# Sorting the tokens of a mixture-of-experts layer in two halves, with gathers and weight loads inside one block loop

## Chip, cores and metric

The kernel runs on one core of one Trainium2 chip. The metric is the time on the device in microseconds (us), median of the runs shown. All arithmetic of the layers is float32. P is 128 throughout.

## What is computed

Sixteen samples x of 128 tokens by 128 features pass through four layers. Cut to the core:

```python
# layer 0: an expert per sample, chosen by an id (8 experts, 128 -> 512 -> 128)
h = gelu(x[b] @ Wi[e] + bi[e]);  r = h @ Wo[e] + bo[e] + x[b]
x = layer_norm(r) * gamma[e] + beta[e]
# layer 1: norm, then norm over tokens scaled and shifted per sample (from a small hypernetwork),
# then a mixture of 8 experts (128 -> 512 -> 128), two per token, added to x
h = film(norm_tokens(layer_norm(x) * ln_g + ln_b))
probs = softmax(h @ router_w);  gates, idx = top_k(probs, 2);  gates /= gates.sum()
x = x + sum_over_k(gates[k] * (relu(h @ w1[idx[k]] + b1[idx[k]]) @ w2[idx[k]] + b2[idx[k]]))
# layer 2: pairs of features rotated by theta and phi of the sample
# layer 3: 128 -> 32, gelu, a 32x32 matrix chosen by an id, 32 -> 128, residual, layer_norm
```

## The kernel before

Four groups of four samples run through layer 0: TensorE multiplies (up, gelu on ScalarE, down), VectorE takes mean and variance, GpSimd raises the variance to the power -0.5 and does scale and shift, VectorE normalises. Norm and film of layer 1 for one group run beside layer 0 of the next. Then logits and the two largest per token (`top2`) on VectorE.

All 2048 tokens, 4096 token-and-expert pairs, are sorted by expert at once: a matmul ranks the pairs (`p_rank`), a scan on VectorE gives each pair a slot, each expert's slots are padded to whole blocks of 128, and a matmul of one-hot tiles (`hot_in`, `hot_blk`) inverts the table: for each of 39 blocks, which row of h goes to which slot (`src_i`), and where its result goes (`dest_i`).

A block is: GpSimd gathers 128 rows of h by index out of device memory (`gather`, line 496, ring of 8, seven ahead), TensorE transposes them (line 869), VectorE copies the transpose and the expert's w1 from a table in SBUF (lines 1285, 1291), TensorE does four up matmuls (two instructions each), ScalarE four relu activations (line 651), TensorE four down matmuls, VectorE adds b2 (line 1298), GpSimd scatters the 128 result rows to their token's place (`scatter`, line 504). Instructions of every matmul helper carry line 710.

When all scatters have landed, eight transfers of 256 KB bring the rows back, two per group. VectorE combines them with the gates and x (lines 1333, 1341), and layer 3 follows group by group, with its variance power on GpSimd (line 519) and the output stored by SyncE. Every engine runs its own list in the order written; semaphores alone join them. The order around the blocks on GpSimd:

```python
            for n in range(AHEAD):
                gather(n)
            for n in range(BLOCKS):
                if n + AHEAD < BLOCKS:
                    gather(n + AHEAD)
                scatter(n)
```

## Time and profile before

| | us |
|---|---|
| median of 3 runs | 268.74 (265.86 to 272.72) |
| span of the profiled execution | 237.1 |
| TensorE busy in it | 187.1 |
| VectorE | 127.9 |
| GpSimd | 125.8 |
| ScalarE | 100.3 |

The record holds no time of the profiled execution itself, only its span, from the first to the last instruction; the median is 31.6 us above that. Busy shares are averages over stages with different limits. Matmuls are pipelined and their ends are modelled, so a busy TensorE is not one at its peak.

### The profile page before, as it was taken

How to read it: one execution, taken by the hardware profiler on the slowest of the kernel's cores; microseconds unless marked ns; L12 is line 12 of the kernel's file. 1: busy time of each engine (PE TensorE's matmuls, PEld its weight loads, DVE VectorE, ACT ScalarE, POOL GpSimd, SP SyncE). 2: the span in 40 equal slices, each digit the busy share in tenths (PEclk: the TensorE clock that was granted, in tenths of full speed). 3: DMA queues.
4: the chain of work that ended last, by engine and by line, in shares of the span. 5: the costliest groups of instructions: out<-in, count | busy, mean ns of one | idle time of the engine just before them, and what ended most of it. 6: DMA issues, size and time to landing. Idle time of an engine off the chain costs nothing.

```text
span 237.1 us, 5140 instructions
## 1 busy us (share of the span) xinstructions
PE 187.1 (79%) x1247; PEld 157.3 (66%) x1248; DVE 127.9 (54%) x540; ACT 100.3 (42%) x297; POOL 125.8 (53%) x133
## 2 busy tenths in 40 slices
PE   6699696998446593989999898888997999789900
PEld 5699495996343462478998787777776884268700
DVE  6101425679977699635776555553332320378761
ACT  3123169568221339135555434444443343025530
POOL 6002363655655002577777777777777774001960
PEclk9999889999755555599999999999999999979955
DMA  5999968931169910011111111111112310940113
GB/s 181 234 340 324 305 182 247 333 112 48 52 204 322 318 44 1 24 47 55 48 49 53 49 44 48 49 55 44 45 56 43 52 43 0 251 106 1 44 44 88
DMA packets 32790, 27.19 MB, mean 115 GB/s; under 512 B 3561, under 2 KB 28282, under 8 KB 32768
## 3 DMA queue, kind: packets, MB, share of 16 engines
q1 hardware_dynamic: 23648, 18.44, 26.1%
q0 software_dynamic: 2496, 4.66, 7.6%
q10 hardware_dynamic: 6624, 3.85, 5.7%
q8 instruction: 8, 0.13, 0.2%
q14 instruction: 14, 0.11, 0.1%
HBM read 22.73 MB, written 4.65 MB: 116 GB/s over the span
## 4 chain that ended last, share of the span: by engine, by line
PE 25%; POOL 22%; issue 17%; DMA 16%; DVE 15%; ACT 3%; ACTq 1%; DVEq 0%; POOLq 0%
PE bank L710 22%; POOL got L496 9%; DMA x_sb<-in_x 9%; POOL expert_rows L504 9%; DMA got<-h_rows,src_i 4%; DVE z L1058 2%; DMA w_place<-expert_rows 2%; POOL rstd L453 2%; DVE nmr L1361 2%; PE bank L717 1%; DVE hot_in L1190 1%; ACT act L597 1%; POOL rs L519 1%; DVE hot_blk L1188 1%; DVE st L1349 1%
## 5 line engine op out<-in xcount | busy, mean ns | idle before, releaser
L651 ACT ACTIVATE rows<-bank,small 128x128 f32<-128x128 f32 x156 | 44.5, 368 | 54.3 <-PE bank L710 54.3
L496 POOL DMA_INDIRECT got<-h_rows,src_i x39 | 38.8, 994 | 18.0 <-issue 9.7
L710 PE MATMUL bank<-gotT,rows 128*128 128x128 f32 x312 | 43.7, 283 | 5.6 <-issue 4.0
L504 POOL DMA_INDIRECT expert_rows<-rows,dest_i x39 | 39.9, 1022 | 12.4 <-issue 11.7
L710 PEld LDWEIGHTS bank<-gotT,rows 128*128 128x128 f32 x312 | 37.8, 191 | 10.8 <-issue 8.3
L710 PE MATMUL bank<-w,rows 128*128 x312 | 43.1, 282 | 1.2 <-issue 0.6
L710 PEld LDWEIGHTS bank<-w,rows 128*128 128x128 f32 x312 | 37.8, 191 | 2.8 <-issue 1.6
L597 ACT ACTIVATE act<-bank,small 128x128 f32<-128x128 f32 x64 | 18.1, 370 | 25.5 <-PE bank L710 25.3
L1298 DVE TENSOR_TENSOR rows<-bank,b_tab 128x128 f32<-128x128 f32 x39 | 11.4, 291 | 31.3 <-PE bank L710 30.3
L453 POOL TENSOR_TENSOR rstd<-veps,minus_half 128x4 f32<-128x4 f32 x12 | 12.3, 1022 | 25.5 <-DVE veps L1048 14.5
L1285 DVE COPY gotT<-bank 128x128 f32<-128x128 f32 x39 | 11.2, 288 | 17.5 <-PE bank L869 17.2
L710 PE MATMUL bank<-w_place,act 128*128 128x128 f32 x128 | 19.2, 298 | 1.4 <-ACT act L597 1.4
L710 PE MATMUL bank<-xT,w_place 128*128 128x128 f32 x128 | 20.0, 308 | 0.0
L710 PEld LDWEIGHTS bank<-xT,w_place 128*128 128x128 f32 x128 | 18.7, 224 | 0.7 <-issue 0.7
L710 PEld LDWEIGHTS bank<-w_place,act 128*128 128x128 f32 x128 | 17.3, 209 | 1.8 <-ACT act L597 1.8
L1291 DVE COPY rows<-w 128x512 f32 x39 | 17.6, 451 | 0.7 <-issue 0.7
L519 POOL TENSOR_TENSOR rs<-ve,minus_half 128x4 f32<-128x4 f32 x4 | 4.1, 1022 | 20.2 <-DVE ve L1354 20.1
L869 PE MATMUL bank<-ident,got 128*128 128x128 f32 x39 | 11.5, 294 | 3.1 <-DMA got<-h_rows,src_i 2.8
L710 PE MATMUL bank<-w,ident 128*128 128x512 f32 x26 | 13.9, 692 | 0.0
L710 PE MATMUL bank<-small,hT 128*128 128x8 f32 x32 | 5.7, 306 | 9.5 <-ACT hT L579 9.5
L1039 DVE BATCH_NORM_STATS2 st<-bank 128x6 f32<-128x128 f32 x32 | 7.1, 284 | 10.8 <-PE bank L710 9.0
L710 PEld LDWEIGHTS bank<-small,hT 128*128 128x128 f32 x32 | 5.5, 260 | 10.3 <-issue 10.3
(197 smaller groups left out, 263.5 us busy)
## 6 DMA issues: line engine op xcount, KB each, us to landing
w_place<-in_l_wi SPq DMA_DIRECT2D x16, 256.0 KB, 4.9
w_place<-in_l_wo SPq DMA_DIRECT2D x16, 256.0 KB, 5.9
w<-in_exp_w SPq DMA_DIRECT2D x16, 256.0 KB, 5.9
rows<-in_l_rows SPq DMA_DIRECT2D x16, 192.0 KB, 5.9
x_sb<-in_x ACTq DMA_DIRECT2D x4, 256.0 KB, 6.4
h_rows<-h_row ACTq DMA_DIRECT2D x4, 256.0 KB, 2.5
w_place<-expert_rows SPq DMA_DIRECT2D x4, 256.0 KB, 5.6
w_place<-expert_rows ACTq DMA_DIRECT2D x4, 256.0 KB, 6.3
```

Of the source, the lines that this page charges most:

```text
L453: g_.tensor_tensor(rstd[:, kind, :], veps[:, kind, :], minus_half[:, 0:GS], ALU.pow)\
L496: g_.indirect_dma_start(got[:, n % RING, :], None, h_dram, bass.IndirectOffsetOnAxis(ap=src_i[:, n:n + 1], axis=0))\
L504: g_.indirect_dma_start(y_dram, bass.IndirectOffsetOnAxis(ap=dest_i[:, n:n + 1], axis=0), y_blk[:, n % 4, :], None, bounds_check=TOPK * NR ...
L519: g_.tensor_tensor(rs3[:, g % 2, :], ve3[:, g % 2, :], minus_half[:, 0:GS], ALU.pow)\
L597: last = a_.activation(act0[:, b % 2, c, :], bank[1 + b % 2][:, c * P:(c + 1) * P], ACT.Gelu, bias=cols[:, bass.ds(e * FC + (R_BI + c), 1)])
L651: last = a_.activation(hid[:, k % 2, c, :], bank[k % 2][:, c * P:(c + 1) * P], ACT.Relu, bias=cols[:, bass.ds(e * FC + (R_B1 + c), 1)])
L710: return t_.matmul(out_, lhsT, rhs, start=start, stop=stop)
L869: t_.transpose(bank[6 + k % 2][:, 0:P], got[:, k % RING, :], ident[:]).then_inc(p_gT, 1)
L1039: do(v_.bn_stats(st[:, kind, k, :], src(k)))
L1285: v_.tensor_copy(gotT[:, n % 2, :], bank[6 + n % 2][:, 0:P]).then_inc(v_gT, 1)
L1291: v_.tensor_copy(w1_now[:, n % 2, :], w1[:, bass.ds(expert[n], 1), :].rearrange("p o f -> p (o f)"))\
L1298: v_.tensor_tensor(y_blk[:, n % 4, :], bank[4 + n % 2][:, 0:D], b2_tab[:, bass.ds(expert.pop(n), 1), :].rearrange("p o d -> p (o d)"), ALU ...
```

## The change

The tokens of samples 0 to 7 and of 8 to 15 become two halves. Each is sorted by itself, with half the rank and one-hot widths, into 23 blocks: 46 in all, for 39. The first half's norm, film, routing and sort are placed between the layer-0 samples of groups 2 and 3; the second half's between the blocks of the first (the `if k ==` steps below; a step k is up of block k, down of block k-1, transpose of block k+2). The normalisation of layer 0 moves wholly to VectorE, scale and shift included, in two passes. The bias of layer 0 comes through a matmul on transposed x. The x loads are issued earlier, and weights, output weights and rows of layer 0 have semaphores of their own.

A block's w1 is fetched from device memory by SyncE, five blocks ahead, into a ring of six; it was copied on VectorE. Its transpose is copied by ScalarE. Its result goes by a plain store of SyncE to its slots; there is no scatter. Later each sample's two rows per token are fetched by an indirect transfer through the slot of the token, two per sample, 32 in all: 16 for the first half between the second half's blocks, 16 behind the last block. Gathers and these fetches are held back until TensorE has done the up matmuls or the transpose of a given step. The table of the inverse (one-hot tiles) is made ahead of the row store and the sine on ScalarE. Layer 3 of the first half runs inside the block loop; the second half in four units of two samples; its per-sample matrices come from a table of 18. The variance power of the last unit uses ScalarE's square root and a Newton step on VectorE. GpSimd no longer scales and shifts the output. The loops with a hardware counter are written out. The warming matmuls ahead of layer 3 go.

```diff
+    HALVES = 2
+    HB = NB // HALVES
+    HG = NG // HALVES
+    KT = TOPK * HB
+    BL = (TOPK * HB * S + E1 * (P - 1)) // P
+    NBLK = HALVES * BL
...
+    RING, YRING, TRING, WRING = 16, 4, 3, 6
+    LEAD = 4
+    BOTH = BL - 4
+    FIRST_ROWS = BL + 2
+    WARM_START = (4, 3, 4)
+    UNITS = [(GS * g, GS) for g in range(HG)] + [(b, 2) for b in range(GS * HG, NB, 2)]
+    NU = len(UNITS)
...
+                load_w0(b)
+                if b == 5:
+                    load_rows0(0)
+                if b == 8:
+                    load_rows0(1)
+                if 11 <= b < 15:
+                    load_w2((b - 11) * E1 // 4, (b - 10) * E1 // 4)
+                if b == 13:
+                    load_rows0(2)
...
+            def load_w1(n):
+                e = sp.value_load(exp_i[0:1, n:n + 1], min_val=0, max_val=E1 - 1)
+                if n >= WRING:
+                    sp.wait_ge(p_u, n - WRING + 1)
+                sp.dma_start(w1_now[:, n % WRING, :], exp_w1[bass.ds(e, 1)].rearrange("o d f -> d (o f)"))\
+                    .then_inc(l_w1[n % WRING], 16)
+            def store_y(n):
+                sp.wait_ge(v_y, n + 1)
+                m = n % BL
...
+            for k in range(NBLK):
+                if k + WRING - 1 == BL:
+                    sp.wait_ge(v_exp, 2)
+                if k >= 1:
+                    store_y(k - 1)
+                if k + WRING - 1 < NBLK:
+                    load_w1(k + WRING - 1)
...
+            def fetch_row(u, t, k):
+                h, j = t // HB, k * HB + t % HB
+                g_.indirect_dma_start(y_in[:, t // GS, k, t % GS, :], None, y_dram[h],
+                                      bass.IndirectOffsetOnAxis(ap=slot_i[:, h, j:j + 1], axis=0))\
+                    .then_inc(l_y[u], 16)
...
+            def beside_up(k):
+                pool.wait_ge(p_u, k + 1)
+            def beside_rows(k):
+                pool.wait_ge(p_gT, min(k + 3, NBLK))
...
+            for n in range(BL):
+                if n >= LEAD:
+                    beside_up(n - LEAD)
+                if n == BOTH:
...
+                    pool.wait_ge(st_h[2], 16)
+                    pool.wait_ge(st_h[3], 16)
...
+                if n > BOTH:
+                    beside_rows(n - LEAD)
+                    gather(BL + n - BOTH - 1)
...
+            ahead = 2 * BL - BOTH - 1
+            first_half = rows_of(0) + rows_of(1)
+            for k in range(BL - LEAD, NBLK - LEAD):
+                if k == FIRST_ROWS:
+                    stored(0)
+                i = k - FIRST_ROWS
+                gathers = 2 if i < 0 else k % 2 if i < 11 else 1
+                if gathers > 0 and ahead < NBLK:
+                    beside_up(k)
+                    gather(ahead)
+                    ahead += 1
+                if gathers > 1 and ahead < NBLK:
+                    beside_rows(k)
+                    gather(ahead)
+                    ahead += 1
+                if 0 <= i < len(first_half):
+                    beside_rows(k)
+                    fetch_row(*first_half[i])
...
+            stored(1)
+            fetch(2)
+            power3(1)
+            fetch(3)
+            fetch(4)
+            power3(2)
+            fetch(5)
+            power3(3)
+            power3(4)
...
+                if k == 0 and g + 2 < NG:
...
+                if b == 10:
+                    film_h(0)
+                if b == 12:
+                    film_h(1)
+                if b == 14:
+                    store_rows(0)
...
+            transposed(0)
+            transposed(1)
+            e = block_expert(0)
+            for k in range(NBLK):
+                hidden(k, e)
+                if k + 1 == BL:
+                    act.wait_ge(v_exp, 2)
+                if k + 1 < NBLK:
+                    e = block_expert(k + 1)
+                if k + 2 < NBLK:
+                    transposed(k + 2)
+                if k == 5:
+                    film_h(2)
+                if k == 6:
+                    film_h(3)
+                if k == 7:
+                    store_rows(2)
+                if k == 8:
+                    store_rows(3)
+                if k == 11:
+                    hot_rows(1)
+                if k == 13:
+                    act.wait_ge(v_smax, 1)
+                    a_.activation(soft[:], soft_in[:], ACT.Exp).then_inc(a_sexp, 1)
...
+                if b == 11:
+                    z_transposes(1)
+                if b == 12:
+                    route(0)
+                if b == 14:
+                    rank(0)
+                    rows_back(0)
+                if b == 15:
+                    rows_back(1)
...
+                if b == 8:
+                    z_transposes(0)
+                if b == 13:
+                    route(1)
...
+            pe.wait_ge(v_l0, NG)
+            rows_T(0)
+            rows_T(1)
+            for k in range(NBLK + 1):
+                if k == BL + 1:
+                    pe.wait_ge(v_exp, 2)
+                if k >= 1:
+                    e = pe.value_load(exp_i[0:1, k - 1:k], min_val=0, max_val=E1 - 1)
+                if k < NBLK:
+                    blk_up(k)
+                if k >= 1:
+                    blk_down(k - 1, e)
+                if k + 2 < NBLK:
+                    rows_T(k + 2)
+                if k == 2:
+                    z_transposes(2)
+                if k == 3:
+                    z_transposes(3)
+                if k == 6:
+                    route(2)
+                    rows_back(2)
+                if k == 7:
+                    route(3)
+                    rows_back(3)
+                if k == 9:
+                    rank(1)
+                if k == 13:
+                    inverse(1)
+                if k == 19:
+                    experts3(2)
+                if k == 20:
+                    experts3(3)
+                if k == 37:
...
+            def l0_centre_scale(g):
+                dve.wait_ge(l_rows0[g], 16 * GS)
+                for k in range(GS):
+                    last = v_.scalar_tensor_tensor(
+                        out=z0[:, g % 2, k, :], in0=down_bank(g)[:, k * P:(k + 1) * P],
+                        scalar=mv[:, 0, g % 2, k, 0:1], in1=rows0[:, GS * g + k, 0, :],
+                        op0=ALU.subtract, op1=ALU.mult)
+                last.then_inc(v_l0, 1)
+            def l0_spread_shift(g):
+                dve.wait_ge(g_rstd[0], g + 1)
+                dve.wait_ge(v_l0, g + 1)
+                for k in range(GS):
+                    do(v_.scalar_tensor_tensor(
+                        out=x1[:, GS * g + k, :], in0=z0[:, g % 2, k, :], scalar=rstd[:, 0, g % 2, k:k + 1],
+                        in1=rows0[:, GS * g + k, 1, :], op0=ALU.mult, op1=ALU.add))
+                settle()
...
+            def last_root():
+                r, v = rs3[:, there(NU - 1)], ve3[:, there(NU - 1)]
+                dve.wait_ge(a_sd3, 1)
+                do(v_.reciprocal(r, sd3[:]))
+                settle()
+                do(v_.tensor_tensor(nr3[:], r, r, ALU.mult))
+                settle()
+                do(v_.tensor_tensor(nr3[:], nr3[:], v, ALU.mult))
+                settle()
+                do(v_.tensor_scalar(nr3[:], nr3[:], -0.5, 1.5, ALU.mult, ALU.add))
+                settle()
+                do(v_.tensor_tensor(r, r, nr3[:], ALU.mult))
+                settle()
...
+            l0_stats(0)
+            l0_centre_scale(0)
+            l0_spread_shift(0)
+            l1_stats(0)
+            l1_norm(0)
+            l0_stats(1)
+            l0_centre_scale(1)
+            l0_spread_shift(1)
+            l1_stats(1)
+            row_stats(0)
+            l1_norm(1)
+            film_gain()
+            film_factors(0)
+            row_stats(1)
+            film_factors(1)
+            l0_stats(2)
+            top2(0)
+            top2(1)
+            count_blocks(0)
+            sort_slots(0)
+            hot_blocks(0)
+            hot_slots(0, 8)
+            dve.wait_ge(p_bias, 1)
+            v_.tensor_copy(bias3[:], q_bias3).then_inc(v_bias, 1)
+            hot_slots(8, KT)
+            block_experts(0)
+            sources(0)
+            l0_centre_scale(2)
+            l0_stats(3)
+            l0_centre_scale(3)
+            l0_spread_shift(2)
+            l1_stats(2)
+            l0_spread_shift(3)
+            l1_stats(3)
+            dve.wait_ge(l_w2, 16 * (E1 + 1))
+            dve.wait_ge(v_exp, 1)
...
+                if k == 1:
+                    l1_norm(2)
+                if k == 2:
+                    l1_norm(3)
+                if k == 3:
+                    row_stats(2)
+                if k == 4:
+                    film_factors(2)
+                    row_stats(3)
+                if k == 5:
+                    film_factors(3)
+                if k == 7:
...
+                if k == 10:
+                    count_blocks(1)
+                if k == 11:
+                    sort_slots(1)
+                    hot_blocks(1)
+                if 12 <= k < 14:
+                    hot_slots(8 * (k - 12), 8 * (k - 11))
+                if k == 12:
```

## Rows read from the trace of the kernel before

**Rows 1.** The page, part 2: 40 slices, busy tenths of TensorE and its granted clock
```profile
PE   6699696998446593989999898888997999789900
...
PEclk9999889999755555599999999999999999979955
```

**Rows 2.** Waits: who waited for whom, total us, times, longest
```profile
PE bank L717 <- DMA x_sb<-in_x: 5.8, 3, 2.2
```

**Rows 3.** Timeline, TensorE: sums of groups 1 and 3 (start us, us, engine, line)
```profile
36.82 1.02 PE L710 MATMUL bank<-x_bo,ident 128*128 128x512 f32 x2
...
58.07 1.02 PE L710 MATMUL bank<-x_bo,ident 128*128 128x512 f32 x2
```

**Rows 4.** Timeline: sort and first gather
```profile
82.71 0.29 PE L710 MATMUL bank<-both,behind 128*128 128x128 bf16 x1 [0.68 <-DVE both L1121]
...
86.83 1.45 DVE L1183 TENSOR_TENSOR hot_tmp<-col_bf,blk_of_bf 128x1248 bf16<-128x1248 bf16 x1
...
90.91 3.33 DVE L1190 TENSOR_SCALAR hot_in<-col_bf,in_blk 128x128 bf16<-128x128 bf16 x20
...
97.04 1.21 POOL L496 DMA_INDIRECT got<-h_rows,src_i  x1 [6.39 <-DVE dest_i L1216]
...
100.27 0.27 PE L869 MATMUL bank<-ident,got 128*128 128x128 f32 x1
```

**Rows 5.** Timeline: the end of the kernel
```profile
196.33 1.15 PE L710 MATMUL bank<-w,rows 128*128 x8 [0.59 <-ACT rows L651]
...
200.97 2.04 SPq L401 DMA_DIRECT2D w_place<-expert_rows  x4
...
226.53 0.17 DVE L1354 TENSOR_SCALAR ve<-mv 128x4 f32<-128x4 f32 x1
...
229.09 0.81 ACT L691 ACTIVATE zg<-bank,nmr,rs 128x128 f32<-128x128 f32 x2 [2.13 <-DVE nmr L1361]
...
231.49 0.69 DVE L1384 TENSOR_TENSOR z<-zg,rows 128x512 f32<-128x512 f32 x1
```

**Rows 6.** Timeline: expert blocks, early and later
```profile
105.65 1.06 PE L710 MATMUL bank<-gotT,rows 128*128 128x128 f32 x8
...
107.55 1.06 PE L710 MATMUL bank<-gotT,rows 128*128 128x128 f32 x8
...
127.91 0.98 POOL L496 DMA_INDIRECT got<-h_rows,src_i  x1 [0.30 <-issue]
...
130.51 0.98 POOL L496 DMA_INDIRECT got<-h_rows,src_i  x1 [0.30 <-issue]
```

**Rows 7.** Windows of 10 us: busy time and instructions of each engine, clock, DMA
```profile
170.00:180.00 10.00, 9.05 (x67) 7.89 (x67) 3.79 (x12) 4.49 (x16) 7.56 (x9) 1.00 0.17 46
```

**Rows 8.** Windows of 1 us, TensorE alone: busy, granted clock, DMA share, GB/s
```profile
26.00:27.00 1.00, 0.00 (x0) 1.00 1.06 339
...
28.00:29.00 1.00, 1.00 (x8) 0.63 0.70 212
...
32.00:33.00 1.00, 1.00 (x11) 1.00 0.14 33
```

**Rows 9.** Groups by line and shape: count | busy us, mean ns | idle before
```profile
L651 ACT ACTIVATE rows<-bank,small 128x128 f32<-128x128 f32 x156 | 44.5, 368 | 54.3 <-PE bank L710 54.3
...
L453 POOL TENSOR_TENSOR rstd<-veps,minus_half 128x4 f32<-128x4 f32 x12 | 12.3, 1022 | 25.5 <-DVE veps L1048 14.5 <-DVE veps L1069 8.4 <-DVE veps L1083 2.4
...
L1039 DVE BATCH_NORM_STATS2 st<-bank 128x6 f32<-128x128 f32 x32 | 7.1, 284 | 10.8 <-PE bank L710 9.0 <-PE bank L783 1.7
...
L579 ACT ACTIVATE hT<-bank,film 128x128 f32<-128x128 f32 x16 | 6.0, 462 | 12.0 <-DVE film L1102 12.0
...
L1333 DVE SCALAR_TENSOR_TENSOR x_bo<-w_place,gates,x 128x128 f32<-128x128 f32 x16 | 4.5, 346 | 7.5 <-DMA w_place<-expert_rows 7.5
```

**Rows 10.** The page, part 6: transfers by issue, KB each, us to landing
```profile
w<-in_exp_w SPq DMA_DIRECT2D x16, 256.0 KB, 5.9
```

**Rows 11.** The tile of gathered rows: landing of its transfers
```profile
DMA to landing us min/median/max: 2.4/2.6/4.2
```

1382 lines of the change are left out of this document (675 added, 707 removed).

## Prediction

> **What bounds the kernel now.** I read the slices of the page first [rows 1]: TensorE is busy nearly everywhere, but from the twelfth slice to the seventeenth its granted clock is 5 tenths, and its busy share swings between 3 and 9. So there are three stretches with different limits, and the change touches all of them.
>
> Stretch 1, start to first gather, 97.0 us. Layer 0 is fed by transfers: TensorE waited 5.8 us in three waits for x [rows 2], and the second group's sum ended at 37.8, the fourth's at 59.1 [rows 3]. Then norms, routing and sort of all 2048 tokens run one behind the other: the rank matmul stands at 82.7, the hot tiles at 86.8 to 94.2, the gather at 97.0 [rows 4]. That is 38 us after layer 0 in which no expert works.
>
> Stretch 2, 39 expert blocks, 97.0 to 197.5 [rows 4, 5]. While the first seven gathers last, a block takes 1.90 us (its up matmuls at 105.65, the next at 107.55) [rows 6]. Later the gathers start 2.60 us apart (127.91, 130.51) [rows 6]: GpSimd issues a gather of 0.98 and a scatter of about the same, each with 0.3 around it. GpSimd is the bound there, although its busy time in 170 to 180 reads only 7.56 of 10 against TensorE's 9.05 [rows 7].
>
> Stretch 3, from the last down matmuls (197.5) to the end of the span (237.1), 39.6 us [rows 5]: scatter, reload of all expert rows (issued at 200.97), layer 3, and from the last output tile (231.49 plus 0.69) 4.9 us of store and end.
>
> **The change, stretch 1.** Groups 0 and 1 get a sort of their own, run during the layer-0 samples of groups 2 and 3. The x loads start earlier and weights are waited for apart from rows. Two of the three x waits lay before the second sum (4.4 us by their mean and maximum), and the half-rate spell between 28 and 32 [rows 8] cost about 1.7; weights ahead of rows, and 128 KB of rows in place of 192 KB, I estimate at 1.7. The second sum so comes at T = 30 in place of 37.8. From there one chain runs through VectorE and GpSimd: statistics of four samples 1.4 (four of 0.284 and the aggregates, [rows 9]), scale on VectorE 1.4 (four of 0.346), shift 1.3, statistics 1.4, the row statistics of group 0 queued in front 2.3, norm 1.1: z1 of group 1 at 39. Transposes 0.6, row statistics 1.5, power 1.2 (1.02 and its wait), factors 0.7, four hT (0.462 each, overlapped) 1.5, logits 1.0, top-2 1.9, waits between engines about 0.6: the rank matmul at 48. TensorE's order puts these steps between samples: at sample 11 it stands some 4 us for z1, at sample 14 some 1.5 us for the top-2, with downs 10 and 13 and all later samples behind it. Layer 0 ends near 53, which is still earlier than 59.1. Rank to hot tiles took 4.1 (3.8 at half the width); hot_tmp has 368 columns for 1248 (0.5 for 1.45); 16 slot tiles at 0.167 make 2.7 (twenty took 3.33); hot tiles to gather 2.8 as now [rows 4]. The sum is 57.8 and the step-by-step one 56.5: I take 57, that is 40 us earlier. Bounds: 52 if no in-order wait bites, 66 if each costs double. Removed with it: the index of the scatter, a product of the hot tiles on VectorE (now on ScalarE, a third as wide, beside the slot tiles) and the scale and shift of layer 0 on GpSimd. VectorE does these in 2.7 where it did a norm pass before; the sums above hold it.
>
> **Stretch 2.** There are 46 blocks, as two sorts pad by themselves. TensorE cannot start one before the last layer-0 tile is scaled (v_l0), which VectorE does behind the sort: 1.4 + 1.4 + 1.4 after the index, and b2 of block 0 comes only after four more such steps, 10 us after it. Behind the waiting TensorE nothing else is queued; behind VectorE's late add stand block 4's transpose, and in the power steps of GpSimd gathers 2, 4 and 5. I put step 4 at 15 us after the first gather. The other 42.5 steps cost 1.93 each (1.90, and a little for the register loads): 82. Scatter and the copy of w1 go, so neither GpSimd (1.3 per gather) nor VectorE holds a step; every step's add and its store through SyncE lie beside the matmuls. TensorE is given work that it did before or behind: routing of groups 2 and 3 (3.2), their z transposes (counted in step 4), rank and inverse 1.5, half of the layer-3 matrices 2.3, and layer 3 of groups 0 and 1 (7.6, from eights at 1.1 and transposes at 0.6): 15. ScalarE has four hidden activations (of 0.368, overlapped some 1.2, [rows 9]) and a copy 0.3 per step; film, hot rows, evacuations and a table load make eight steps longer by 0.5 to 2: 8. Hot slots of VectorE in front of the inverse: 2. Clock at the start: 2. Together 12. End of the last down: 57 + 15 + 82 + 15 + 12 = 181 (197.5 now). The twelve is bounded by 4 and 24.
> The w1 stream (256 KB per block) has no row in such a place. Its landing took 5.9 us in a saturated stretch [rows 10]; it is asked for five steps, 9.6 us, ahead, and SyncE issues two transfers a step of about 0.5 each (four took 2.04, [rows 5]). So nothing from below, and up to 1 us a step if landings doubled. I take nothing. The gather of block n leaves after up n-4; up to its transpose lie 2 × 1.93 + 0.89 = 4.75. Landing is 2.6, at most 4.2, from a point near the end of issue [rows 11]; start to use was 3.23 in the first one (97.04 to the transpose at 100.27) [rows 4]. It fits, by about one microsecond. In the second half the gathers run up to 13 ahead.
>
> **Stretch 3.** Last add, store and landing 3.5 (197.5 to 200.97 now, when the reload is issued). Then GpSimd issues 16 row fetches of 1.28 (20.5) and two power steps (2.2) between; the last lands 1.9 after its issue ends: 28.1. The last unit has two samples: combine 1.4, transpose and copy 0.9, down 0.7, gelu 0.5, up 1.1 at half rate, statistics 0.9: 5.5. From variance to norm 2.56 now (226.53 to 229.09, [rows 5]), with a power of 1.02 and an nmr held beside GpSimd; by Sqrt, five short VectorE operations and nmr 1.8. Norm 0.7, scale and shift 1.1, store and end 4.9. Sum 42.1: 2.5 us longer than now, though half of layer 3 is already done; fetching by token eats it. Bounds 39 and 48.
> Here the Trainium skill speaks against the change (DMA: Bandwidth & Descriptors, section Bandwidth): batch transfers to 1 MiB or more, as each has about 2 us fixed. By its fit (2.0 us and bytes over 436 GB/s) 64 KB would be 2.15 each; one after another 34 us for sixteen, so 14 more than my sum. The rows show two indirect transfers leaving in 2.60 us while each needs 2.6 to land, so they overlap, and I don't follow the rule.
>
> **Rivals.** The bound for telling from no change is 2%, 5.4 us.
> (a) The in-order waits hold the first sort: TensorE stands at samples 11 to 14 and the index comes at 70. For it: six engine changes in the chain, each with TensorE behind it. Against: in the trace the same steps take the times above. +13 us: 268.
> (b) Gathers lengthen beside w1. With each landing at the maximum of 4.2 for 2.6, release to use becomes about 5.1, and a step (5.1 - 0.89) / 2 = 2.1, 0.17 more over 19 steps, 3 us: 258. For it: the margin is thin, and one landing of 4.2 came without any w1 beside it. Against: 39 landings have a median of 2.6. The Trainium skill (DMA: Bandwidth & Descriptors, section Latency and other measured facts) gives HBM access as 0.2 us on average and 2 us at high load; by that the sum would be 260, and no row here has a gather under load.
> (c) Fetches do not overlap in the tail: sixteen at a landing of 2.6 are 41.6 for 20.5, so +21: 276. Against it: two indirect transfers leave in 2.60 [rows 6].
> That is the batching rule above as a mechanism; by the fit of the Trainium skill it would be 269.
> (d) Slower: the clock stays at half through the first blocks. It was at half in 28 to 29, after TensorE had stood idle in 26 to 27, and full again in 32 to 33 [rows 8], yet stayed at 5 tenths for six slices of patchy work [rows 1]. The first blocks are patchy. Each block at half rate costs 1.8 more; from 11 such blocks (14 + 5.4 over 1.8) it decides for slower; through the first half, 19 blocks, 34 us: 289. Against: a block stage at half rate has no gaps, and in such work the clock came back within 4 us.
> (e) The waits of 12 us are hidden, and the first sort is at 54: 244.
>
> **How the numbers follow.** 181 + 42 = 223 for the span, 14 less than 237.1. The record has the span of the profiled execution, not its own time; the median of the three runs is 268.74, 31.6 more, which I leave unchanged: 268.7 - 14 = 255. Chances: this 0.62 (its own range 247 to 264), (e) 0.12, (b) 0.08, (a) 0.09, (c) 0.03, (d) 0.06. Faster by over 2% (below 263.4) takes (e), (b) and all but 0.05 of the forecast: 0.77; slower takes (c) and (d), 0.09; the rest, 0.14, is within 2%. The range 243 to 269 leaves out (c), (d) and a little at either end.
>
> **What would show it.** In the changed profile: first gather near 57 and rank near 48; TensorE idle before the z transposes of group 1 near sample 11; block steps of 1.9 to 2.0 where nothing is inserted; last down near 181; GpSimd solid with indirect transfers of 1.28 for 20 us behind it; 42 us from last down to end. The prediction is wrong if the first gather stands beyond 66, if steps without insertion take 2.3, or if the granted clock reads 5 in the block slices.

## The result, and the profile after

| | us |
|---|---|
| kernel before, median of 4 runs | 267.68 (265.86 to 272.72) |
| kernel after, median of 4 runs | 242.83 (239.67 to 244.58) |
| after to before | 0.906, 95% interval 0.897 to 0.915 |
| span of the profiled execution, before | 237.1 |
| span of the profiled execution, after (its own time 244.58) | 242.8 |

The change makes the kernel 9.4% faster. Yet its profiled span is 5.7 us longer than the one that the prediction rests on. After, time and span differ by 1.8 us; before, by some 30. That is the first thing to explain.

The page of the kernel after, part 2, its 40 slices: busy tenths of each engine and TensorE's granted clock (a slice is 6.1 us).

```profile
PE   6999949899599988859888787998899993068670
...
POOL 4113252114834613333665765665631203877210
PEclk9999979997769979967999999999997998555555
```

The stretch of patchy work at half clock in slices 12 to 17 of [rows 1] is gone. TensorE is busy to slice 33, then waits, at half clock, to the end.

The timeline of the kernel after, in the places of [rows 3], [rows 4] and [rows 5]: start, duration, engine, line. First the second group's sum, the rank matmul, the hot tiles, the index, the first gather and its transpose:

```profile
28.30 0.39 PE L790 MATMUL bank<-ident,xbT 128*128 128x128 f32 x2
...
48.56 0.19 PE L790 MATMUL bank<-both,ones_bf 128*128 128x64 bf16 x1
...
51.77 0.54 DVE L1288 TENSOR_TENSOR hot_tmp<-col_bf,blk_of_bf 128x368 bf16<-128x368 bf16 x1
...
57.13 0.18 DVE L1315 SCALAR_TENSOR_TENSOR src_i<-bank,src_p 128x23 int32<-128x23 f32 x1
...
57.61 1.19 POOL L485 DMA_INDIRECT got<-h_rows,src_i  x1 [4.42 <-DVE src_i L1315]
...
60.92 0.30 PE L953 MATMUL bank<-ident,got 128*128 128x128 f32 x1
```

Rank matmul and first gather stand at 48.6 and 57.6; the prediction had 48 and 57. Before, the gather stood at 97.04 [rows 4]. The up matmuls of step 4 start at 74.99, where 72 was forecast. Then the other end:

```profile
199.90 1.06 PE L790 MATMUL bank<-w,hid 128*128 x8
...
203.76 1.02 POOL L496 DMA_INDIRECT w_place<-slot_rows,slot_i  x1 [13.25 <-DMA slot_rows<-y_blk]
...
224.72 0.95 POOL L496 DMA_INDIRECT w_place<-slot_rows,slot_i  x1 [0.30 <-issue]
...
237.15 0.17 DVE L1399 TENSOR_SCALAR ve<-mv 128x2 f32<-128x2 f32 x1
...
238.78 0.81 ACT L727 ACTIVATE zg<-bank,nmr,rs 128x128 f32<-128x128 f32 x2 [1.22 <-DVE nmr L1420]
...
240.08 0.42 DVE L1431 TENSOR_TENSOR z<-zg,rows 128x256 f32<-128x256 f32 x1
```

The last down ends at 201.0, not at 181. From there to the end it is 41.8 us, where the prediction had 42.1. So the first and the third stretch came as worked out, and the blocks took 17 us more than forecast (126 for 109, from step 4 on).

In windows (busy us and instructions of each engine, granted clock, DMA share), the counterpart of [rows 7]:

```profile
140.00:150.00 10.00, 7.33 (x57) 6.33 (x56) 3.24 (x7) 4.24 (x16) 6.28 (x7) 1.00 0.53 152
150.00:160.00 10.00, 9.33 (x75) 8.35 (x74) 2.36 (x6) 5.46 (x20) 5.45 (x6) 1.00 0.55 172
...
205.00:225.00 20.00, 9.48 (x30) 5.93 (x30) 8.40 (x35) 3.88 (x10) 15.76 (x17) 0.50 0.29 80
```

From 120 to 180 the clock is full and no engine is full: TensorE has 7.3 of 10 us in one window and 9.3 in the next, GpSimd 6.3 and 5.5. The transposes of block 19 and block 40 start at 118.8 and 176.9: 21 steps in 58.0 us, 2.76 each. In steps with nothing in their way the same trace shows 1.95 to 2.1. What TensorE waits for there can be seen in one place:

```profile
140.00 0.27 PE L953 MATMUL bank<-ident,got 128*128 128x128 f32 x1
140.09 0.95 POOL L485 DMA_INDIRECT got<-h_rows,src_i  x1 [0.30 <-issue]
...
140.37 1.13 PE L790 MATMUL bank<-gotT,w_now 128*128 128x128 f32 x8
141.93 0.28 ACT L694 ACTIVATE gotT<-bank 128x128 f32<-128x128 f32 x1 [2.14 <-remote]
142.00 0.29 DVE L1369 TENSOR_TENSOR y_blk<-bank,b_tab 128x128 f32<-128x128 f32 x1 [3.10 <-remote]
...
142.16 0.95 POOL L485 DMA_INDIRECT got<-h_rows,src_i  x1 [1.12 <-PE bank L790]
```

The transpose is over at 140.27. ScalarE, which has nothing else to do, takes it up at 141.93, VectorE starts the add of the block before at 142.00, and GpSimd its next gather at 142.16. Three engines start within 0.25 us, and what freed them, to the profile, is "remote" or a matmul ended long ago. The trace also records each update of a semaphore, which the lines shown here leave out. TensorE's three (down, transpose, up) are recorded at 141.87, 141.91 and 142.00, though their matmuls end, by the model, at 140.16, 140.27 and 141.50. I call an update late if it comes over 0.1 us after the modelled end. The Trainium skill (Perfetto Trace Analysis, section Per-instruction lifecycle: what the profiler-reported window actually captures) says that a matmul's end is worked out from its size, and that its semaphore update is pushed only when PSUM has acknowledged the write. The rows agree that the two can part; how far is what these traces add.

Counted in this way over the blocks (updates that the trace lacks left out):

| execution | TensorE updates | late | sum of lateness us | longest |
|---|---|---|---|---|
| before, the profiled one of the prediction | 116 | 0 | 0 | |
| before, profiled again | 104 | 43 | 105.3 | 5.47 |
| after | 135 | 40 | 37.0 | 2.14 |
| after, in 113 to 177 alone | 63 | 37 | 35.5 | 2.14 |

Where the trace lacks an update, the next one can be taken for it. If each is given to the last matmul that ended before it, the kernel before profiled again has 41 of 106 late, 99.0 us in sum, and the kernel after is as in the table: the counts hold to a few. A second sign does not depend on them: the engine that waits for the update starts just behind it, as above.

### The profile page after: what moved, and what is told of

The parts are those of the page before. It is cut to its first block, busy times and chain, and to the rows that moved or that the text cites. A ratio compares the mean times of both kernels' runs of the same rounds, so it can differ in the third digit from the quotient of the medians.

```text
span 242.8 us, 5763 instructions
## 1 busy us (share of the span) xinstructions
PE 193.2 (80%) x1390; PEld 172.5 (71%) x1390; DVE 106.4 (44%) x512; ACT 118.7 (49%) x373; POOL 101.2 (42%) x117
## 4 chain that ended last, share of the span: by engine, by line
PE 57%; issue 10%; ACT 9%; DVE 8%; DMA 7%; POOL 4%; another core or an unknown queue 1%; ACTq 1%; SPq 1%; DVEq 0%; POOLq 0%
PE bank L790 51%; DMA got<-h_rows,src_i 3%; PE bank L953 3%; ACT hid L704 2%; DMA w_place<-in_l_wi 2%; POOL w_place L496 2%; POOL rstd L470 1%; ACT gotT L694 1%; DVE hot_in L1295 1%; DVE st L1158 1%; PE bank L981 1%; ACT zg L727 1%; POOL got L485 1%; DMA ids<-in_ids 1%
## 5 line engine op out<-in xcount | busy, mean ns | idle before, releaser
L704 ACT ACTIVATE hid<-bank,small 128x128 f32<-128x128 f32 x184 | 52.5, 370 | 44.1 <-PE bank L790 39.5
L790 PE MATMUL bank<-w,hid 128*128 x368 | 53.6, 292 | 9.9 <-ACT gotT L694 4.3
L790 PE MATMUL bank<-gotT,w_now 128*128 128x128 f32 x368 | 55.0, 297 | 4.0 <-issue 1.6
L790 PEld LDWEIGHTS bank<-w,hid 128*128 128x128 f32 x368 | 48.1, 204 | 12.6 <-issue 12.5
L790 PEld LDWEIGHTS bank<-gotT,w_now 128*128 128x128 f32 x368 | 48.6, 206 | 9.2 <-issue 7.5
L1369 DVE TENSOR_TENSOR y_blk<-bank,b_tab 128x128 f32<-128x128 f32 x46 | 13.4, 291 | 80.8 <-PE bank L790 70.5
L496 POOL DMA_INDIRECT w_place<-slot_rows,slot_i x32 | 31.2, 976 | 36.6 <-PE bank L953 17.5
L694 ACT ACTIVATE gotT<-bank 128x128 f32<-128x128 f32 x46 | 13.0, 282 | 19.4 <-PE bank L953 10.9
L790 PE MATMUL bank<-xT,w_place 128*128 128x128 f32 x128 | 17.4, 280 | 0.6 <-DMA w_place<-in_l_wi 0.6
L790 PE MATMUL bank<-m,a 33*128 x32 | 9.8, 405 | 2.0 <-issue 1.5
L981 PEld LDWEIGHTS bank<-ident,xbT 128*128 128x128 f32 x16 | 2.3, 163 | 11.5 <-issue 11.5
L953 PEld LDWEIGHTS bank<-ident,got 128*128 128x128 f32 x46 | 7.0, 151 | 4.9 <-DMA got<-h_rows,src_i 4.7
```

Source lines behind the costliest of these rows:

```text
L496: g_.indirect_dma_start(y_in[:, t // GS, k, t % GS, :], None, y_dram[h], bass.IndirectOffsetOnAxis(ap=slot_i[:, h, j:j + 1], axis=0))\
L694: a_.activation(gotT[:, n % TRING, :], got_bank(n), ACT.Copy).then_inc(a_gT, 1)
L704: last = a_.activation(hid[:, n % 2, c, :], up_bank(n)[:, c * P:(c + 1) * P], ACT.Relu, bias=cols[:, bass.ds(e * FC + (R_B1 + c), 1)])
L790: return t_.matmul(out_, lhsT, rhs, start=start, stop=stop)
L953: t_.transpose(got_bank(n), got[:, n % RING, :], ident[:]).then_inc(p_gT, 1)
L981: last = t_.transpose(uT_bank[u][:, k * P:(k + 1) * P], u_b[:, place(u) + k, :], ident[:])
```

## The experiments

Theory from the traces: TensorE's updates come late beside GpSimd's indirect transfers when these follow each other closely. The change is faster not only by its earlier start but as it has fewer late updates; the prediction did not see them, as the one profile it had held none.

### The kernel before again

Two kernels: before unchanged (e1_before_alone), and before with its two hardware loops written out:

```diff
-            with act.Fori(0, LOOPS) as turn:
+            for turn in range(LOOPS):
-            with pe.Fori(0, LOOPS) as turn:
+            for turn in range(LOOPS):
```

> The kernel before, unchanged, so that each of its executions shows its own span. The prediction took 31.6 us outside the span as a constant of every kernel. Theory A: the 31.6 us belong to this program (span 237, time 265 to 269, so 29 to 32 us outside). Theory B: they belong to no program; the one profiled execution was quicker than the timed ones, whose spans lie near 265 (under 3 us outside).

> The kernel before with its two hardware loops (TensorE's and ScalarE's, three turns of eight blocks each) written out as 24 blocks; nothing else. Theory A1: what lies outside the span is the cost of the hardware loops in an execution that is not profiled; time 239 to 245. Theory A2: it is a cost of the program as a whole, of its scatters or its eight large loads; time stays at 264 to 270. If the order of the loops costs nothing either way, the span stays at 237 within 3 us.

Measured: 271.1 us (269.1 to 274.8, ten executions), each with its span: 267.1 to 271.9. Written out: 266.1 us, ratio to before 0.988 (0.984 to 0.993), profiled span 265.0. Theory B holds for the first: nothing lies outside the span but 2 to 3 us, and the execution of 237.1 was the exception. With the runs below, the spans of 65 executions of the kernel before are on record, on two chips: 264.0 to 273.9, none near 237. Written out, the loops give some 1%, not 30 us. Page part 2 of the new profile of before:

```profile
PE   6797979980748586965783873969296599969910
...
POOL 5011636645611265574654654756465524301670
```

Transposes of blocks 0 and 38 start 126.1 us apart (98.66, 224.74); in the profile of the prediction 91.2. The missing 30 us lie here. One gap of its timeline:

```profile
118.59 0.27 PE L869 MATMUL bank<-ident,got 128*128 128x128 f32 x1
...
119.25 0.97 POOL L496 DMA_INDIRECT got<-h_rows,src_i  x1 [0.31 <-issue]
...
120.52 1.01 POOL L504 DMA_INDIRECT expert_rows<-rows,dest_i  x1 [0.30 <-issue]
121.84 0.97 POOL L496 DMA_INDIRECT got<-h_rows,src_i  x1 [0.30 <-issue]
124.03 0.29 DVE L1285 COPY gotT<-bank 128x128 f32<-128x128 f32 x1 [3.58 <-remote]
...
124.45 0.79 PE L710 MATMUL bank<-gotT,rows 128*128 128x128 f32 x2 [4.69 <-DVE gotT L1285]
```

The transpose ends at 118.86; its copy on VectorE starts at 124.03, and TensorE stands 4.69 us. Meanwhile GpSimd issues three transfers with 0.3 us between. It stops as the next scatter waits for VectorE's rows, and then everything goes on. Such gaps of 7 to 8 us from one transpose to the next recur every six to eight blocks.

### Without w1's stream, without pacing, without fetches in the loop

```diff
# e3_w1_six_loads
-                if k + WRING - 1 < NBLK:
+                if k + WRING - 1 < WRING:
                     load_w1(k + WRING - 1)
#   and TensorE's waits for the loads left out
# e4_no_pacing
             def beside_up(k):
-                pool.wait_ge(p_u, k + 1)
+                pass
             def beside_rows(k):
-                pool.wait_ge(p_gT, min(k + 3, NBLK))
+                pass
# e7_no_fetch_in_loop
-                if 0 <= i < len(first_half):
+                if False:
#   and VectorE's waits for these fetches
```

> The kernel after, with the w1 loads of the blocks 6 to 45 left out (each block multiplies by what the first six loads brought), so 40 transfers of 256 KB fewer. In the kernel after, steps 20 to 43 take 2.9 us each where undisturbed ones take 2.0, and TensorE's semaphore updates come 0.5 to 1.7 us after the modelled end of their matmuls there. Theory X: the stream of w1 beside GpSimd's transfers makes these updates late; steps fall to 2.0 to 2.2 us, time falls by 12 to 18 us. Rival Y: GpSimd's own transfers do it, whatever SyncE's queue carries; time stays within 3 us. Rival Z: half of each, 5 to 9 us.

> The kernel after without the waits that pace GpSimd's transfers by TensorE's up matmuls and transposes (the wait for a free place in the ring of 16 stays). Theory X: late updates come where a GpSimd transfer stands 0.3 us behind another; without pacing more of them do, and the steps up to block 30 get slower: time up by 3 to 10 us. Rival Y: pacing only holds gathers back; rows come earlier, the steps that waited for a transfer (some 4 us in all) no longer do: time down by 2 to 5 us. Rival N: nothing changes (within 2 us), as GpSimd is ahead anyway.

> The kernel after with the 16 fetches of the first half inside the loop left out (the combine takes what stands in the tile), so steps 25 to 40 have one GpSimd transfer or none. Theory G: these steps go from 2.5 us on average to 2.0 to 2.1, time falls by 5 to 9 us. Rival Q (another limit, as the add on VectorE or the stores, sets 2.25 us): the steps stay at 2.25 and over, time falls by under 3 us.

Measured, where "19 to 40" is the time between the transposes of those blocks:

| | time us | ratio to before | 19 to 40 us | late updates |
|---|---|---|---|---|
| after, on the same chip (e17 below) | 245.96 | 0.912 (0.905 to 0.919) | 59.0 | 44 |
| w1 six loads | 244.88 | 0.913 (0.905 to 0.922) | 58.5 | 41 |
| no pacing | 283.45 | 1.054 (1.044 to 1.064) | 88.5 | 21, longest 13.64 |
| no fetches in loop | 239.2 | 0.879 (0.870 to 0.887) | 54.5 | 24 |

Theory X of the first fell: 40 transfers of 256 KB fewer, and nothing changes. Pacing is the large piece: without it the kernel is slower than before, 37.5 us above itself on the same chip, far beyond the 3 to 10 that I expected. Its late updates are fewer (21 for 44), but their lateness adds up to 124 us for 42. Its timeline near the start of a row of gathers:

```profile
122.13 0.27 PE L953 MATMUL bank<-ident,got 128*128 128x128 f32 x1
...
122.43 1.13 PE L790 MATMUL bank<-gotT,w_now 128*128 128x128 f32 x8
122.65 0.96 POOL L485 DMA_INDIRECT got<-h_rows,src_i  x1 [0.31 <-issue]
123.91 0.96 POOL L485 DMA_INDIRECT got<-h_rows,src_i  x1 [0.30 <-issue]
125.17 0.95 POOL L485 DMA_INDIRECT got<-h_rows,src_i  x1 [0.30 <-issue]
...
126.43 0.95 POOL L485 DMA_INDIRECT got<-h_rows,src_i  x1 [0.30 <-issue]
127.33 0.28 ACT L694 ACTIVATE gotT<-bank 128x128 f32<-128x128 f32 x1 [4.63 <-remote]
```

GpSimd issues 16 gathers in a row from 120.1 to 140.0. The transpose of 122.13 is copied at 127.33; the next one starts at 129.3, the one behind it only at 145.5, the second largest gap (the largest is 16.3, beside another such row). Windows of the same kernel:

```profile
120.00:140.00 20.00, 7.07 (x45) 6.20 (x43) 0.58 (x2) 3.32 (x13) 15.30 (x16) 0.79 0.39 97
...
200.00:220.00 20.00, 19.62 (x161) 17.92 (x160) 4.90 (x17) 12.26 (x43) 0.00 (x0) 1.00 0.54 150
```

The busier GpSimd (15.3 of 20), the idler TensorE (7.1); once its gathers are done (200 to 220) steps take 2.1. Without fetches in the loop the stretch of 147 to 171, where GpSimd is busy 5 us of 20, has 27 updates and none late, at 2.1 a step; the stretch before it (113 to 147), with two transfers a step as ever, has 21 late of 31. That is Theory G, and it is worth 6 us (blocks 19 to 45 take 68.9 us where the kernel after, on this chip, takes 75.2).

### Gaps between transfers, and pacing alone

```diff
# e5_no_pacing_gaps: no pacing, and behind each gather and in-loop fetch
# e11_paced_with_gaps: paced as in after; one memset, from gather 16 on
+                for _ in range(3):        # e11: once
+                    ch.do(g_.memset(filler[:], 0.0))
+                    ch.settle()
# e6_before_paced (the kernel before)
                 if n + AHEAD < BLOCKS:
+                    pool.wait_ge(p_u, n + 1)
                     gather(n + AHEAD)
+                pool.wait_ge(p_gT, min(n + 3, BLOCKS))
                 scatter(n)
# e14_lead_of_eight
-    LEAD = 4
+    LEAD = 8
...
-            for k in range(BL - LEAD, NBLK - LEAD):
+            for k in range(BL - LEAD, NBLK - 4):
```

> The kernel after without pacing (as in the run without pacing, 283.45 us), but with three small memsets on GpSimd, each waited for, behind every gather and every fetch of the first half. They cost GpSimd some 0.6 us a transfer and give TensorE nothing. Theory G (updates of the other engines' semaphores are held while GpSimd issues one transfer 0.3 us behind the other, and go through in a gap): time falls from 283 to 245 to 262, and no step lasts over 8 us. Rival P (only a wait of GpSimd for TensorE's progress helps, or GpSimd's rate itself decides): time stays at 283 or rises by up to 10 us, with steps of 11 to 16 us as without the memsets.

> The kernel before with the pacing alone: a gather waits for the block's up matmuls, a scatter for the transpose two blocks later. Theory G: the blocks lose part of the 34 us by which a usual execution of the kernel before is longer than its first profiled one; time 269 falls to 245 to 260. Rival P: GpSimd has two transfers of 1.3 us in every step, so waits only delay it; time rises to 270 to 285.

> The kernel after with one memset of 128x256 (some 0.4 us with its wait) on GpSimd behind each gather from block 16 on and behind each fetch inside the loop. Theory G': two transfers in a step no longer stand 0.3 us behind each other, TensorE's updates come in time, and steps 20 to 43 fall from 2.6 to 2.2 us: time 2 to 8 us below the kernel after. Rival P (GpSimd's own rate sets these steps: 36 transfers in 22 steps; 0.4 us more for each): 3 to 12 us above.

> The kernel after with gathers eight blocks ahead of the block's up matmuls in place of four (constant LEAD), so that some 8 transfers move out of steps 15 to 23 into the first steps, where GpSimd has idle time. Theory G': fewer steps carry two transfers, at 0.5 to 1.0 us each: time 2 to 5 us below the kernel after. Rival: GpSimd waits in order for the second sort's hot tiles and index, so the transfers only bunch behind these; time within 2 us, or up to 4 us above.

> The kernel after, unchanged, on the same chip as the others: 240 to 246 us, ratio to the kernel before 0.90 to 0.92.

| | time us | ratio to before | late, longest |
|---|---|---|---|
| e5, no pacing, gaps | 275.68 | 1.018 (1.012 to 1.024) | 0 of 110 |
| e6, before, paced | 272.79 | 1.006 (1.001 to 1.012) | 43 of 106, 5.53 |
| e11, paced, gaps | 246.84 (242.75 to 248.7) | | 52 of 131, 2.26 |
| e14, lead of eight | 260.37 | 0.956 (0.946 to 0.966) | 19 of 129, 8.83 |
| e17, after | 245.96 (243.24 to 247.84) | 0.912 (0.905 to 0.919) | 44 of 131, 2.25 |

Gaps of about 1.4 us behind each transfer (2.4 us from one to the next) take every late update away, and the steps from 27 to 38 run at 2.1. But time fell by 8 us only, not by 21: GpSimd is now too slow, and VectorE, whose list has the combine of unit 0 at step 35, waits for its rows:

```profile
DVE z L1386 <- DMA w_place<-slot_rows,slot_i: 31.4, 3, 20.8
```

So Theory G was right on the updates and wrong on the time; a wait of the program took their place. Three memsets cost GpSimd 1.2 us a transfer, twice what I had put down. In the kernel after, one memset (1.55 us from one transfer to the next) is no gain: as many late updates, same time. That is neither theory of e11: 0.3 us more do not free the updates, and as they cost no time either, GpSimd's own rate does not set these steps (Rival P). Pacing the kernel before does nothing either, as Rival P of e6 had it. Its GpSimd has two transfers in every step, so a wait only moves them. That pacing works in the kernel after because a step there has one or two is my reading; no run shows it by itself. A lead of eight lets rows of 7 and 11 transfers through, and costs some 12 us (ratio 0.956 for 0.912), with two steps of 11.5: my expectation that emptier steps would take them was the wrong way round.

### The same with nothing around it

Three kernels of their own, which hand tiles from TensorE to ScalarE and back:

```python
for n in range(ROUNDS):                       # TensorE, e10_dense_ping_pong
    pe.wait_ge(a_c, n - 1)                    # two rounds ahead of ScalarE
    for c in range(4):                        # e9_ping_pong: one transpose, not ahead
        last = matmul(bank[n % 4][:, c * P:(c + 1) * P], w_t[:], ident[:])
    last.then_inc(p_t, 1)
for first, many in GROUPS:                    # GpSimd
    pool.wait_ge(p_t, first)
    for i in range(many):
        indirect_dma_start(got[:, i, :], None, rows, ...).then_inc(gat[i], 16)
```

> A kernel of its own: TensorE and ScalarE hand a 128x128 tile to and fro 330 times (some 0.75 us a round), while GpSimd issues 1, 2, 3, 4, 8, 12 and 16 gathers of 128 rows in a row, then three times 8 gathers with 1, 3 and 6 memsets of 128x256 between them; no other transfer runs. Theory G: rounds beside one gather last 0.75 us, beside n gathers in a row one round lasts up to n x 1.3 us; memsets between them bring the rounds back under 3 us. Rival D (the late updates need the other transfers, w1 and the stores, beside GpSimd's): every round lasts 0.75 to 1 us.

> A kernel of its own, as the first ping-pong, but TensorE does four 128x128 float32 matmuls a round and is two rounds ahead of ScalarE, so it is busy all the time (some 0.95 us a round, 240 rounds). GpSimd issues 1, 2, 4, 8 and 16 gathers in a row; from round 120 SyncE also stores 64 KB every second round, beside 2, 4, 8 gathers in a row and then 12 with a memset of 128x256 behind each. Theory G' (TensorE's semaphore updates come late when it is busy and GpSimd issues one transfer 0.3 us behind another): rounds beside the rows of 4 to 16 gathers last 2 us and more, beside single gathers and those with a memset 0.95. Rival D (the stores are needed as well): only the rounds from 120 on are longer. Rival E (neither: it needs more of the kernel): all rounds 0.95 to 1.1 us.

> The dense ping-pong again, in five stretches: (1) four float32 matmuls of 128 columns a round beside 8 powers in a row on GpSimd; (2) the same beside 8 gathers in a row (in the dense ping-pong: rounds of up to 3.3 us in place of 0.89); (3) one float32 matmul of 512 columns a round, as long but a quarter of the instructions, beside 8 gathers; (4) four bfloat16 matmuls, a quarter of the time, beside 8 gathers; (5) two float32 matmuls a round beside 8 gathers. Theory I (number of TensorE's instructions a microsecond): stretch 2 and 4 have late updates of 0.6 us and more, stretch 3 none, stretch 1 none. Theory B (TensorE's busy time): 2 and 3 have them alike, 4 fewer, 1 none. Rival O (any GpSimd operations in a row): stretch 1 has them too.

In e9 every round takes 0.84 us, beside 16 gathers in a row too, so close transfers alone do nothing. In e10 the round of 0.89 us becomes 2.1 beside 4 gathers in a row, 3.3 beside 8, and 8.5 beside 16; one gather leaves no mark, nor do two. The largest:

```profile
90.98 2.07 PE L74 MATMUL bank<-ident,w_t 128*128 128x128 f32 x8 [2.22 <-ACT a_t L81]
...
95.25 0.95 POOL L56 DMA_INDIRECT got<-in_x,idx  x1 [0.30 <-issue]
96.50 0.94 POOL L56 DMA_INDIRECT got<-in_x,idx  x1 [0.30 <-issue]
99.11 0.28 ACT L81 ACTIVATE a_t<-bank 128x128 f32<-128x128 f32 x1 [8.19 <-remote]
```

TensorE's matmuls end near 93.05; the update is recorded 6.04 us later, and ScalarE takes up at 99.11, 1.7 us after the last gather's end. Stores of SyncE beside it change little (3.9 us beside 8 gathers), and beside 12 gathers with a memset behind each (1.44 us from one to the next) rounds still take up to 2.2, where I had expected 0.95. Windows of e15, by what TensorE does: four float32 matmuls beside powers, the same beside gathers, one matmul of 512 columns, four in bfloat16, two float32:

```profile
15.00:40.00 25.00, 25.00 (x227) 25.00 (x226) 7.76 (x28) 8.10 (x8) 1.00 0.01 1
43.00:54.00 11.00, 7.82 (x66) 7.25 (x64) 1.94 (x7) 7.33 (x8) 0.95 0.17 50
94.00:103.00 9.00, 9.00 (x22) 3.84 (x22) 3.05 (x11) 6.87 (x8) 1.00 0.18 51
127.00:137.00 10.00, 4.99 (x48) 3.07 (x47) 2.73 (x11) 7.35 (x8) 0.72 0.15 46
161.00:171.00 10.00, 7.33 (x46) 5.92 (x44) 2.78 (x11) 6.87 (x8) 0.89 0.18 54
```

Powers in a row on GpSimd (8.1 us) leave TensorE full. Beside gathers it falls to 7.8 of 11, and a round of 0.89 us takes up to 3.7; with bfloat16 one of 0.43 up to 2.1, with two matmuls one of 0.63 up to 2.9. With one matmul of 512 columns every round keeps its 0.86, ScalarE takes up each within 0.05 us, and TensorE stays full (22 instructions in 9 us; undisturbed, the rounds of four have 227 in 25). So it takes indirect transfers, close behind each other, and many TensorE instructions a microsecond: 9.1 undisturbed in the rounds of four, 2.4 with 512 columns, 1.2 in e9. Busy time alone is not it, and Theory I holds. As each matmul here has its weight load, these runs don't tell matmuls and weight loads apart.

### Other parts of the change

```diff
# e8_last_root_gpsimd
-                    last_root()
+                    dve.wait_ge(g_rstd3, u + 1)      # and power3(5) on GpSimd
# e12_tiles_behind_sine (ScalarE)
-            hot_rows(0)
             store_rows(1)
...
             evac_m3(0)
+            act.wait_ge(v_arg, 1)
+            a_.activation(trig[:], arg[:], ACT.Sin).then_inc(a_trig, 1)
+            hot_rows(0)
             evac_m3(1)
...
-            act.wait_ge(v_arg, 1)
-            a_.activation(trig[:], arg[:], ACT.Sin).then_inc(a_trig, 1)
# e13_warm_tail (TensorE)
             for u in range(2, NU):
+                for v in used_by(o3_bank, u):
+                    pe.wait_ge(a_z3, v + 1)
+                keep_warm(36 if u == 2 else 3, o3_bank[u], ident[:])
                 l3_T(u)
```

> The kernel after with the last variance root back on GpSimd (power -0.5 as for the other units) in place of ScalarE's square root and VectorE's seven small operations. From the last variance to the last normalisation it takes 1.63 us in the kernel after; a power on GpSimd takes 0.7 to 1.0 us, with some 0.25 us of semaphores either side. My theory: time changes by less than 1 us (1.6 against 1.3 to 1.6 us). Rival: VectorE's chain was worth it, time rises by 1 to 2 us.

> The kernel after with ScalarE's tile of the first inverse behind the rows of group 1, one table of layer 3 and the sine, in place of ahead of them. My theory: the first gather starts later by the work put ahead of it, 0.57 + 0.57 us, and a table load of 1.28 us with a sine of some 0.5 us, so 2 to 3 us, and the time rises by as much (245 to 246). Rival: VectorE's hot tiles end 3.3 us later than ScalarE's anyway, so nothing moves (under 1 us).

> The kernel after with 36 matmuls without use on TensorE behind the last block, where it waits 10 us for the fetches of unit 2 at half clock, and 3 more ahead of each later unit. In the kernel after the units of the tail follow each other every 5.0 us on TensorE, of which 4.3 is work at half clock, and the last transposes start 5 us behind the last fetch's issue. Theory W: with the clock at full, a unit takes 3 us of TensorE, the tail ends 2 to 5 us sooner (238 to 241). Rival: GpSimd's fetches pace the tail (four of 1.25 us a unit), and the matmuls delay the first unit: within 1 us, or up to 2 us slower.

These three ran on another chip than e17, so they are compared by their ratios to the kernel before on their own chip (the kernel after has 0.912, or 0.906 in its first runs). The last root on GpSimd: 246.31 us, ratio 0.917 (0.904 to 0.929), as the kernel after within the intervals. The chain itself is shorter:

```profile
238.25 0.17 DVE L1397 TENSOR_SCALAR ve<-mv 128x2 f32<-128x2 f32 x1
238.50 0.69 POOL L509 TENSOR_TENSOR rs<-ve,minus_half 128x2 f32<-128x2 f32 x1 [4.35 <-DVE ve L1397]
...
239.42 0.81 ACT L728 ACTIVATE zg<-bank,nmr,rs 128x128 f32<-128x128 f32 x2 [3.61 <-DVE nmr L1415]
```

1.17 us from variance to norm where the kernel after takes 1.63 (237.15 to 238.78). This part of the change loses 0.5 us, too little to time.

The tiles behind the sine: 245.64 us, ratio 0.917 (0.903 to 0.931), again the same. ScalarE's tile came at 57.37 in place of 52.39, TensorE stood 2.94 us for it, and the first gather started at 59.74. But the transpose of block 4 started at 71.8, as in the kernel after (72.0): the first steps wait for something behind the sort, not for the rows; by the order of its list it is VectorE's work. Two microseconds on the chain of the first gather are given back by block 4.

The warm tail: 248.1 us, ratio 0.924 (0.912 to 0.936), so not faster, and by its ratio some 1% slower, within the intervals. The clock went up as meant, and came down again:

```profile
216.15 0.62 PE L790 MATMUL bank<-xT,dw_rot 128*32 128x128 f32 x4 [1.08 <-issue]
...
220.82 0.63 PE L981 MATMUL bank<-ident,xbT 128*128 128x128 f32 x2
...
223.73 0.38 ACT L712 ACTIVATE xT<-bank 128x256 f32<-128x256 f32 x1 [6.46 <-remote]
...
224.17 1.06 PE L790 MATMUL bank<-xT,dw_rot 128*32 128x128 f32 x4 [2.71 <-issue]
```

The second unit's down takes 0.62 in place of 1.06 us. Then the transposes of 220.82, among matmuls without use and beside fetches in a row, are taken up at 223.73 (their update is 2.26 late), TensorE stands, and the next down takes 1.06 again. None of the kernels run beats the kernel after but the one that leaves the fetches out.

## Why the prediction was right and wrong

- **First gather at 57, rank at 48:** right (57.6, 48.6). The second sum came at 28.7, not 30; z transposes of group 1 at 39.5, as added up (two x waits by their mean and maximum are 4.1 us, not 4.4). But the stands lay elsewhere: TensorE stood 3.48 us before that, up to 33.9, on ScalarE's four table loads, which the sum left out, and not at all ahead of the z transposes, where 4 were forecast; for the top-2 it was 0.64, not 1.5.
- **Step 4 at 15 us after it:** 17.4.
- **42.5 steps of 1.93, "82", extras 15, stalls 12:** this is the term that failed, 109 forecast and 126 measured. The price of 1.93 was right for an undisturbed step (1.95). Blocks 19 to 40 cost 2.76 each, 17.0 us above 1.95 each, of which 2.3 are extra matmuls that the 15 held; the other steps are some 26 above 1.95 each, near the 27 of extras and stalls. What was missing in the 17 is a wait for late updates: 37 of 63 are late there. Shown by a run are 6 us (e7); no run took all of them away and kept the rest as it was, so for the others the link is read from the trace. The bound of 24 for the stalls fell short too.
- **w1 costs nothing:** right (e3). Rival (b), slow gathers beside w1, is out with it: the higher latency that the Trainium skill gives for high load (DMA: Bandwidth & Descriptors, section Latency and other measured facts) did not show at this load: 244.88 us without 40 of the loads, 245.96 with them.
- **Rival (d), half clock through the first blocks:** out; the slices of the blocks read 6 to 9 tenths, from 120 to 180 us full clock.
- **The tail at 42.1:** 41.8. Fetches leave every 1.25 us. Rival (c), fetches one after another, did not come true. The last root was forecast at 1.8 and took 1.6, but is no gain over GpSimd's 1.2.
- **"31.6 more, which I leave unchanged":** the second step that failed, and the larger. It was no constant: 1.8 us in the kernel after, 2 to 3 in the kernel before. The profile was that of an execution without late updates, with a span that none of the 65 others came near. In a usual one the span before is near 266; the prediction set its 223, a span without late updates, against 237.1, another, and then added 31.6 to it.
- The sum: span 223 + 17 (blocks) + 3 (first steps) = 243, and 1.8 outside it, for 31.6: 244.6, the time of the profiled execution. Two misses of 20 and 30 with opposite signs left 255 against 242.83; that they cancel in part is luck. Rival (e), at 244, has the number but not the mechanism: its sort at 54 and its hidden waits did not happen.
- **GpSimd "holds no step":** wrong in kind. It holds them not by its rate but by what its transfers do to TensorE's updates.
- **Where the gain comes from:** first gather to last down is 143 us in the kernel after for 46 blocks (3.1 each), and 135 (95.4 to 230.3) in an ordinary execution of the kernel before for 39 (3.5 each); it starts 38 us sooner, and the tail is 41.8 for 39.3. So the gain of 26.8 us between these two spans is the 37.8 of the earlier start, less 8.4 for seven more blocks and 2.5 for the tail. Pacing is needed to keep it: without it all is lost. It reads "waits" in the profile, and the prediction gave it no price at all.

Open: why one execution of the kernel before had none of this. Its 78 transfers stood as close as ever, one every 1.30 us from 97 to 199, beside the same matmuls, and no update was late. So close transfers beside dense matmuls, which bring lateness on in the other profiles, are not enough by themselves: something that these runs did not vary must be there too. Its trace lacks 2 of the blocks' updates, the next one 13 of 117, so the recording may be strained by the same traffic or have a part in it. That lateness goes with the number of TensorE's instructions, each of which leaves its record in the trace, would fit this rival too. Every execution with a span was recorded, and no run here tells these apart. Why the updates are late inside the chip was not settled either, only what brings it on in these executions.

## What to carry to other kernels

Subtract a profile only from an execution of the same kind: if time and span of the profiled kernel are 30 us apart, that is the first thing to explain, not a constant. Where engines all start within a quarter of a microsecond on an event that ended long ago, look at what GpSimd does: spread its indirect transfers so that no row of them stands beside dense small matmuls, and pace them by TensorE's own progress. A longer lead is not safer: here eight blocks in place of four cost 12 us. And where a recorded event seems late, look whether the engine that waits for it started late as well: a record that is missing looks the same.

## What the runs showed of the hardware that was not expected

- Semaphore updates of TensorE up to 6 us late beside 16 indirect transfers of 0.94 us issued 0.3 us apart, in a kernel with nothing else in it; none beside one or two transfers, beside powers on GpSimd, with one small transpose every 0.84 us, or with one matmul of 512 columns every 0.86 us.
- In the kernel after, 1.4 us between transfers, without pacing, takes the late updates away (0 of 110); 0.6 us, with pacing, does not (52 of 131).
- The Trainium skill (SBUF — State Buffer, section SBUF: two separate sides) has contention the other way round, VectorE holding GpSimd from writing descriptors, and says of SBUF's engine ports that TensorE never waits on anyone. Here GpSimd's transfers kept their 0.95 us, and TensorE's updates were late. These runs don't say which port or path it is.
